# SyncE holds back the weights of the next attention until the routed rows are fetched, and an expert's last third of rows is written first

## What is computed

```
x = x + L0_gnn(layernorm(x))
x = x + L0_ffn(layernorm(x))      # 8 routed experts of 768 inner values, top 2, and one shared expert of 384
x = x + L1_gnn(layernorm(x))      # graph attention, 12 heads
x = x + L1_ffn(layernorm(x))      # self-attention (c_attn, c_proj), then 8 experts of 3072 inner values
x = x + L2_gnn; x = x + L2_ffn; x = x + L3_gnn
x = x + L3_ffn(layernorm(x))      # attention, 8 routed experts of 384, top 2, and a shared expert

L0_ffn: probs = softmax(x @ router_w); gates, idx = top_k(probs, 2); gates /= sum(gates)
        expert e: (silu(x @ w_gate[e]) * (x @ w_up[e])) @ w_down[e]
        routed = sum over the token's two experts of gate * expert(x)
        out = alpha * shared + (1 - alpha) * routed,  alpha = sigmoid(x @ sg_w + sg_b)
```

## Time and profile before

| | us |
|---|---|
| runs | 1784.74 median (1781.89 to 1790.84) |
| profiled execution, time | 1785.15 |
| profiled execution, span on the core | 1783.3 |
| TensorE busy | 1669.1 (94%) |
| VectorE busy | 617.0 (35%) |
| ScalarE busy | 442.6 (25%) |
| granted TensorE clock, mean | 0.979 |

### The profile page before, as it was taken

The page is one execution under the profiler, slowest core; times in us unless marked ns, Lnnn a source line. Parts: engine busy times, 40 slices in busy tenths (PEclk is TensorE's granted clock), DMA queues, the critical chain, the costliest instruction groups (busy, mean ns, idle before and its releaser), DMA issues.

```text
span 1783.3 us, 27162 instructions
## 1 busy us (share of the span) xinstructions
PE 1669.1 (94%) x11992; PEld 987.5 (55%) x11992; DVE 617.0 (35%) x1116; ACT 442.6 (25%) x818; POOL 47.8 (3%) x53
## 2 busy tenths in 40 slices
PE   7999999999999999499999988888999999999998
PEld 4675445664466555377654433333566554777754
DVE  4414995029972211361420000001323142233122
ACT  0013884038851111151310000000521010131121
POOL 0000000000000000100000000000002000000000
PEclk9999999999999999689999999999899999999999
DMA  9225986329756995702489999999535329130594
GB/s 394 101 91 157 214 227 235 130 84 220 221 196 240 393 392 231 309 1 107 163 322 388 422 428 429 429 429 428 248 125 215 146 80 362 69 144 28 202 371 169
DMA packets 85485, 425.17 MB, mean 238 GB/s; under 512 B 10744, under 2 KB 51216, under 8 KB 63680
## 3 DMA queue, kind: packets, MB, share of 16 engines
q1 hardware_dynamic: 79504, 410.67, 61.0%
q10 hardware_dynamic: 4576, 6.39, 1.1%
q0 software_dynamic: 1280, 6.29, 1.0%
HBM read 409.89 MB, written 15.73 MB: 239 GB/s over the span
## 4 chain that ended last, share of the span: by engine, by line
PE 77%; DMA 16%; DVE 4%; issue 1%; ACT 1%; SPq 0%; POOL 0%; DVEq 0%; POOLq 0%; ACTq 0%
PE banks L117 74%; DMA weight_ring<-in_L_ffn_c_fc_dram 8%; PE banks L120 3%; DMA weight_ring<-in_L_ffn_c_proj_e_dram 2%; DMA weight_ring<-in_L_gnn_W_in_dram 2%; DMA r_chosen<-expert_rows,r_index 1%; DVE weight_ring L123 1%; DMA gate_queries<-in_L_gnn_query_rep_dram 1%; DMA node_parts<-gate_node_parts 1%; DMA r_rows<-slot_rows 1%; DVE stat L276 1%; DMA gate_rows<-node_parts 1%; SPq L157 0%; DVE x_tok L134 0%; DMA expert_rows<-r_outB 0%
## 5 line engine op out<-in xcount | busy, mean ns | idle before, releaser
L117 PE MATMUL banks<-weight_ring,xT 128*128 128x384 f32 x864 | 293.5, 491 | 1.5 <-DVE rgat_xr L140 1.5
L123 DVE TENSOR_TENSOR weight_ring<-weight_ring,gate_queries 128x1024 f32<-128x1024 f32 x192 | 222.8, 1222 | 19.6 <-ACT weight_ring L151 12.0
L117 PEld LDWEIGHTS banks<-weight_ring,xT 128*128 128x128 f32 x864 | 162.3, 191 | 108.6 <-issue 8.8
L151 ACT ACTIVATE weight_ring<-banks 128x1024 f32<-128x1024 f32 x192 | 190.9, 1024 | 43.7 <-PE banks L117 40.5
L117 PE MATMUL banks<-xT,weight_ring 128*128 128x256 f32 x792 | 180.7, 383 | 3.2 <-ACT x_tok L154 3.2
L117 PEld LDWEIGHTS banks<-xT,weight_ring 128*128 128x128 f32 x792 | 151.7, 192 | 28.0 <-issue 3.6
L117 PE MATMUL banks<-weight_ring,r_xd 128*32 128x384 f32 (+1 forms) x2304 | 145.2, 407 | 0.0
L117 PE MATMUL banks<-weight_ring,moe_xdT 128*64 128x384 f32 x720 | 123.4, 493 | 21.3 <-DMA weight_ring<-in_L_ffn_c_fc_dram 21.3
L117 PE MATMUL banks<-gate_rows,selrow 96*128 96x512 bf16 x384 | 107.4, 381 | 3.3 <-ACT weight_ring L151 1.8
L117 PEld LDWEIGHTS banks<-weight_ring,r_xd 128*32 128x32 f32 x2304 | 73.2, 110 | 61.5 <-issue 50.7
L117 PE MATMUL banks<-weight_ring,selrow 128*32 128x256 f32 x1536 | 102.2, 385 | 3.3 <-DVE weight_ring L123 3.2
(11 more groups left out here) (372 smaller groups left out, 1730.2 us busy)
## 6 DMA issues: line engine op xcount, KB each, us to landing
weight_ring<-in_L_ffn_c_fc_dram SPq DMA_DIRECT2D x30, 2304.0 KB, 26.0
weight_ring<-in_L_ffn_c_proj_e_dram SPq DMA_DIRECT2D x21, 2304.0 KB, 28.3
gate_queries<-in_L_gnn_query_rep_dram SPq DMA_DIRECT2D x48, 512.0 KB, 5.2
weight_slot_heads<-in_L_ffn_c_proj_e_dram SPq DMA_DIRECT2D x9, 2304.0 KB, 28.7
weight_ring<-in_L_ffn_w_gate_dram SPq DMA_DIRECT2D x8, 2304.0 KB, 15.4
weight_ring<-in_L_ffn_w_up_dram SPq DMA_DIRECT2D x8, 2304.0 KB, 14.7
weight_ring<-in_L_ffn_w_down_dram SPq DMA_DIRECT2D x8, 2304.0 KB, 15.2
weight_ring<-in_L_ffn_w_dram SPq DMA_DIRECT2D x16, 1152.0 KB, 7.9
```

What stands on the lines that cost most here:

```text
L117: return self.e.matmul(out, lhsT, rhs, start=start, stop=stop)
L123: return self.e.tensor_tensor(out, a, b, op)
L151: return self.e.activation(out, a, f, **kw)
```

## The change

`expert_rows_sp` (both routed stages) now writes `outB` first, as soon as VectorE has copied it, and waits for the rest of the expert's output only before it writes `outA`. For this the second `outB` copy gets an increment of its own. In L0_ffn, SyncE waits for both chunks' fetch before it goes on to the branch and to L1_ffn's loads.

```
         def expert_rows_sp(q, B, e):
             s, z, r = B["stage"], e % 2, e % 4
+            q.wait_ge(*at("expert_out_dve", (s, e, "last third")))
+            q.dma(dram["expert_rows"][NARROW * e + SLOT:NARROW * (e + 1), :], B["outB"][THIRD * r:THIRD * (r + 1), :]
+                  ).then_inc(*mark(f"expert_rows_{z}", (s, e), 16))
             wait_expert_out(q, B, e)
             q.dma(dram["expert_rows"][NARROW * e:NARROW * e + SLOT, :], B["outA"][SLOT * z:SLOT * (z + 1), :]
-                  ).then_inc(*mark(f"expert_rows_{z}", (s, e), 16))
-            q.dma(dram["expert_rows"][NARROW * e + SLOT:NARROW * (e + 1), :], B["outB"][THIRD * r:THIRD * (r + 1), :]
                   ).then_inc(*mark(f"expert_rows_{z}", (s, e), 16))
...
             for i in range(2):
-                v.cp(outB[own, i * HALF:(i + 1) * HALF], PS[(2 + i) * THIRD:(3 + i) * THIRD, 7, 0:HALF])
+                t = v.cp(outB[own, i * HALF:(i + 1) * HALF], PS[(2 + i) * THIRD:(3 + i) * THIRD, 7, 0:HALF])
+            t.then_inc(*mark("expert_out_dve", (s, e, "last third")))
             if e % 2:
...
             expert_rows_sp(q, R0, last - 1)
             expert_rows_sp(q, R0, last)
+            for c in range(TC):
+                q.wait_ge(*at(f"rows_chosen_{c}", "r0"))
             taken_branch(q, R0, over_sp)
```

## The result

The changed kernel takes 1767.13 us (median of 6 runs, 1761.1 to 1771.97), against 1783.11 us for the kernel before (median of 6). The ratio is 0.9913, with a 95% interval of 0.9896 to 0.993, which is 12 to 19 us, 15.5 at the middle. The forecast was 1771.1 in a range of 1767 to 1777, so the median lies only just inside its lower end. Of the 4 us between forecast and median, 1.6 are the kernel before, whose median was 1784.74 when I predicted; the rest is gain above the 13.6 us that I had summed.

A forecast was written before the change was run, and what follows sets the result against it. L0_ffn's end was taken to be set by the expert-row fetch, stretched by the weight stream. Gains of 12.17 + 0.57 + 0.9 = 13.6 us off the 1784.74 us median gave 1771.1 us, range 1767 to 1777.

The forecast's parts named there:

- The fetch (12.17 us): L0_ffn: without weights beside it, first fetch issue to VectorE's chunk 1 falls from 21.01 to 8.84 us, as in L3_ffn.
- The moved loads cost nothing: L1_ffn's five loads, issued behind the fetch, still land before use; 51 us of cover for the first c_attn matrix.
- The gain lasts: After L0_ffn: later DMA-bound work starts when TensorE frees slots and moves with it, so the gain carries through whole.
- The write order in L0_ffn (0.57 us): Expert 7, L0_ffn: outB written before outA makes the last landing 713.84 instead of 714.41, and GpSimd's fetch follows.
- The write order in L3_ffn (0.9 us): L3_ffn's end: with outA written last, the final landing comes 0.5 to 1.4 us sooner; 0.9 taken, counting fully.
- TensorE's groups back to back: Adding rows after L0_ffn's fetch: chunk 1's matmuls may wait or gain from the clock; zero taken, 0.9 us either way.
- The pause at the jump (kept at 4.10): TensorE's jump over L0_ffn's overflow body falls into the weight stream again: 4.10 us kept, at most about 2.5 to gain.
- The clock (plus or minus 3): TensorE restarts around L1_gnn: 2.9 to 8.8 us at 1.2 GHz after each, so plus or minus 3 us on the sum.
- the slow fetch: Rival: L0_ffn's fetch is slow by itself, so only the write order's 1.5 us is gained, 1783.2 us; chance 0.03.
- the gain given back: Rival: L1_ffn's expert streams end at a set time, losing all but L3_ffn's 0.9 us, 1783.8 us; chance 0.03.
- the low clock: Rival: TensorE stays at the low clock through L1_gnn, 27 us more work, 1798 us; chance 0.02.
- The code fetch behind the weights: Rival: in L1_gnn's beginning, instruction waits beside the stream cost 2.5 us each; two leave 8.6 us gain, 1776.1; chance 0.06.

The follow-up runs named there:

- second profile: The changed kernel executed again, unaltered, as the measure for a held run on the same chip: 1768.27 us, ratio 0.9925.
- the run that takes the cover away: Changed kernel with the weights held until the transposes at L1_gnn's end, about 3 us ahead of c_attn's first matmul: 1768.42 us, ratio 0.9915.
- held past the turn or the jump: Changed kernel, weights held until L1_gnn's transposes on TensorE (1764.77 us, again 1762.58) or only its first L1_gnn matmuls behind the jump (1765.51 us).
- the missing jump: Changed kernel without L0_ffn's overflow branch on any engine: 1762.38 us, ratio 0.9878.
- the run with three matrices ahead: Changed kernel with all three c_attn loads issued ahead of the wait for the fetch: 1780.55 us, executed once.

## Why the prediction was right, step by step

- **The fetch (12.17 us).** Right in mechanism and size: 12.7 us in the changed kernel, 12.63 in its second profile, 12.6 with the wait alone. L3_ffn's fetch was the right measure, if a little long. The estimate by the Trainium skill ("DMA: Bandwidth & Descriptors", Anatomy of one DMA), about 14 us of gain, was too high by more than a microsecond; the chunk's second transfer took 4.66 us in the chain after, not 2.9.
- **The moved loads cost nothing.** Right: no wait on a c_attn or c_fc matrix before 1000 us, and the run that takes the cover away has one of 7.62 us.
- **The gain lasts.** Right within the spread of one execution: from c_attn to L3_ffn's last copies it is 955.0 us before and 955.5 and 952.6 after.
- **The write order in L0_ffn (0.57 us).** 0.65 and 0.66. I had missed that it depends on the wait: alone it is lost in the fetch.
- **The write order in L3_ffn (0.9 us).** The tail is 1.06 and 1.47 us shorter, 1.31 with the order alone. Over all ten runs with the new order it is 20.93 to 22.44, against 22.87 and 22.83 without, so single executions spread by more than the term.
- **TensorE's groups back to back.** Chunk 0 and 1 ran as one group of 5.49 us from 720.22 to 725.70. Chunk 1's start to "issue" is 5.34 us, for 5.05 before: 0.3 us lost. In the second profile the group took 4.30 us and the same stretch 4.14: 0.9 us gained. Both are inside the 0.9 either way that I gave.
- **The pause at the jump (kept at 4.10).** Right for this kernel, 4.19 and 5.08. The reason was the one that I gave, the stream runs over it again; that 2.2 to 3.9 us of it are the stream's price (4.19 and 5.08 against 1.23 to 2.02 in quiet) and can be had back by a later release was no part of the forecast, and the runs show it. The 2.5 us that I gave as the most to be had there were too little: chunk 1 to the transposes is 2.9 to 4.6 us shorter in the three runs held past the turn or the jump, in part because the 10 matmuls behind the jump took under 2 us instead of 3.27 in two of them.
- **The clock (plus or minus 3).** The stretch from the transposes to c_attn took 54.4 to 54.7 us in three runs and 56.9 to 57.9 in seven others (the late hold and the missing jump aside). The first profile of the changed kernel has the short one, the second the long one. In the first, the clock was back at 753.2 after TensorE's restart at 750.12, and the 216 matmuls behind it took 34.55 us. In the kernel before it came back only at 774.1 after 765.27, and the same 216 took 37.25. The second profile of the changed kernel goes past the 8.8 us that I had for the longest spell: back at 761.2 after 749.38, and 38.62 us for the 216.

The sum of 13.6 us stands against 15.5 (12 to 19) timed. By the table, from the copy to the end, the two profiles of the changed kernel are 15.8 and 16.2 us shorter than the one before. The terms that I summed make 14.4 and 14.8 of this (0.65 + 12.70 + 1.06, and 0.66 + 12.63 + 1.47). The rest lies in stretches that differ by as much between executions of like kernels: to c_attn (-2.3 and +0.9) and the rest (+0.5 and -2.4). Whether any of it belongs to the change I can't tell.

Of the rivals, the slow fetch, the gain given back and the low clock are excluded by these runs. The code fetch behind the weights is half true: one such transfer is delayed, at the jump, and it was delayed before as well (it began 6.6 us after chunk 1), so it took next to nothing from the gain.

**A version that is faster still.** Holding the weights until TensorE is past its jump or its transposes keeps the whole gain and adds to it. The 18 runs of the three held kernels average 1764.0 us, the 12 of the changed kernel 1767.7. The difference of 3.6 has a standard error of 1.5 from the spread of the runs, and the profiles agree with it: chunk 1 to the transposes is 2.9 us shorter in the least case and 4.6 in the largest. The single intervals against the kernel before overlap, so it is likely rather than certain. Whether the jump taken out would give more is not shown: its six runs average 1761.5 us, 2.5 below the held ones with a standard error of 1.6, while its stretch from chunk 1 to c_attn is no shorter than in the two held past the turn. It is needed anyway, for tokens that find no slot.

## What to carry to other kernels

A short transfer on the path that runs beside a long one is slowed while both last: here 8.3 us became 20.4 with 11 us of stream left beside it, and 21.0 with more than it could outlast. Look for the same transfer elsewhere in the trace without company: its time there is what you can get. If the long one's first use is far off, let the issuing engine wait for the short one's semaphore, and release it behind the next jump as well, since a jump may be waiting for a transfer of its own (2.2 to 3.9 us here).

## What the runs showed of the hardware that I had not expected

- The pause behind TensorE's jump goes with the DMA engines' load: 1.23 to 2.02 us in quiet, 4.02 to 5.08 beside a stream, and 6.37 in the run with three matrices ahead, where two packets of the instruction queue begin in the pause instead of one (from 740.1 to 740.5 us); why two, I can't tell. The Trainium skill ("Runtime: NRT & Kernel Launch", Instruction fetch mechanics) says that a jump out of the loaded window stalls for a transfer; the runs agree, and show that such a transfer begins some 3 us later beside the weights.
- The slowing of a fetch by weights ahead of it is far from proportional: 1.4 us for one matrix (5.5 us of stream), 12.1 for three, 12.7 for five. It goes by what is left of them when the fetch's rows begin to move.
- L1_gnn's stretch to c_attn ran in one of two lengths, about 54.6 or 57.5 us, by how long the low clock lasted after a restart (3.1 to 4.6 us in the three short ones, 8.9 to 11.8 in the seven long ones). I found nothing in the kernels that chooses between them.
